# Filling TensorE's waits around normalizations and attention openings with products of resident constants

## The reference

```python
x = L0(x, ctx, ctx, mask)   # 16 heads of 64: softmax(q k^T / 8) v, out projection, + x
x = L1(x, ctx)              # gated fusion with the pooled ctx, then a layer normalization
x = L2(x, ctx, ctx)         # 16 heads of 16, relu projections, causal mask; normalization
x = L3(x, ctx)              # banded self-attention (window 64, per-head slopes) + norm,
                            # full cross-attention with ctx + norm, gelu feed-forward + norm
```

## Time and profile before

| | us |
|---|---|
| median of 3 runs | 1954.51 |
| lowest and highest | 1943.39, 1956.11 |
| the profiled execution | 1960.79 |
| its span (first to last instruction) | 1958.8 |
| TensorE matmuls busy | 1569.5 (80%) |
| TensorE weight loads busy | 829.0 (42%) |
| DVE busy | 939.8 (48%) |
| ACT busy | 736.4 (38%) |
| POOL busy | 253.6 (13%) |
| mean granted TensorE clock | 0.848 of full |

### The profile page before, as it was taken

One profiled execution on the slowest core, in us unless ns is written; L12 is line 12 of the kernel. 1 busy time (PEld: TensorE's weight loads), 2 busy tenths in 40 slices (PEclk: granted clock), 3 DMA queues, 4 the chain that ended last, 5 costly groups with the idle time before them and its releaser, 6 DMA issues.

```text
span 1958.8 us, 25869 instructions
## 1 busy us (share of the span) xinstructions
PE 1569.5 (80%) x8920; PEld 829.0 (42%) x8920; DVE 939.8 (48%) x2240; ACT 736.4 (38%) x1281; POOL 253.6 (13%) x116
## 2 busy tenths in 40 slices
PE   5998876688998887668899878676889987848686
PEld 2235544334424544533532554452353255536234
DVE  2654554461465464456155355445516626535551
ACT  1642333263263242427246215143524621514352
POOL 1012110200101211110010311120010031112001
PEclk9998787778999878867999877785899997879688
DMA  8001103402100211240210030223111012031200
GB/s 303 1 6 33 33 11 56 97 1 102 45 1 6 44 22 28 40 96 1 102 45 1 6 59 7 45 54 65 64 50 34 1 22 49 1 61 42 50 22 11
DMA packets 44860, 84.04 MB, mean 43 GB/s; under 512 B 10416, under 2 KB 28592, under 8 KB 44464
## 3 DMA queue, kind: packets, MB, share of 16 engines
q1 hardware_dynamic: 44288, 78.42, 17.0%
q10 hardware_dynamic: 432, 3.83, 0.5%
HBM read 42.37 MB, written 2.10 MB: 23 GB/s over the span
## 4 chain that ended last, share of the span: by engine, by line
PE 40%; issue 27%; DVE 18%; ACT 7%; SPq 4%; POOL 1%; DMA 1%; DVEq 0%; ACTq 0%; POOLq 0%
PE ring L1008 8%; DVE nmax L894 7%; PE ring L1029 5%; PE obank L1237 5%; PE ring L1218 4%; PE ring L1272 3%; DVE region_d L778 3%; ACT region_e L595 2%; SPq L377 2%; PE ring L1020 2%; ACT region_e L671 2%; SPq L370 2%; PE ring L1187 2%; PE ring L1039 2%; PE ring L1109 2%
## 5 line engine op out<-in xcount | busy, mean ns | idle before, releaser
L894 DVE TENSOR_REDUCE nmax<-ring 128x2 f32<-128x1024 f32 (+4 forms) x384 | 308.5, 852 | 253.3 <-PE ring L1187 179.5
L671 ACT ACTIVATE region_e<-ring 128x1024 f32<-128x1024 f32 (+4 forms) x384 | 267.4, 734 | 231.7 <-PE ring L1187 110.3
L778 DVE CUSTOM_DVE_ANT_0 region_d<-ring,maskb 128x512 f32<-128x512 f32 x256 | 165.7, 686 | 118.1 <-issue 117.8
L595 ACT ACTIVATE region_e<-region_d,nmin 128x512 f32<-128x512 f32 x256 | 182.6, 714 | 92.1 <-DVE nmin L778 86.1
L1187 PE MATMUL ring<-cbf 64*128 64x128 bf16 (+1 forms) x2048 | 177.4, 260 | 0.0
L663 ACT ACTIVATE q_all<-ring 2x1024 fp32r<-2x1024 bf16 x96 | 97.5, 1016 | 197.7 <-PE ring L1248 196.7
L1201 PE MATMUL ring<-k_tiles_a,q_all 64*128 64x512 f32 (+4 forms) x384 | 108.1, 578 | 65.6 <-DMA q_all<-q_parts 47.0
L1218 PE MATMUL ring<-q_all,k_tiles_a 64*128 64x512 f32 (+4 forms) x384 | 101.5, 531 | 72.6 <-ACT region_e L671 50.9
L1067 PE MATMUL obank<-region_e,vs 128*64 128x512 f32 x512 | 139.9, 630 | 15.1 <-DVE vs L764 15.1
L1057 PE MATMUL ring<-region_q 64*128 64x512 f32 x512 | 141.3, 636 | 5.4 <-ACT region_q L584 5.4
L529 POOL TENSOR_TENSOR nat_x<-nat_n,rows 128x1024 f32<-128x1024 f32 x16 | 39.0, 2439 | 641.6 <-DVE nat_n L859 641.6
(11 more groups left out here) (167 smaller groups left out, 2282.0 us busy)
## 6 DMA issues: line engine op xcount, KB each, us to landing
q_all<-q_parts SPq DMA_DIRECT2D x288, 64.0 KB, 2.3
k_tiles_a<-k_parts SPq DMA_DIRECT2D x144, 64.0 KB, 2.3
k_tiles_b<-k_parts SPq DMA_DIRECT2D x144, 64.0 KB, 2.3
region_b<-in_w_f SPq DMA_DIRECT2D x8, 1024.0 KB, 5.2
wvo<-in_wv SPq DMA_DIRECT2D x4, 1024.0 KB, 8.1
wqk<-in_wq SPq DMA_DIRECT2D x4, 1024.0 KB, 10.0
wqk<-in_wk SPq DMA_DIRECT2D x4, 1024.0 KB, 12.0
wvo<-in_wo SPq DMA_DIRECT2D x4, 1024.0 KB, 5.5
```

Source lines behind the costliest of these rows:

```text
L595: ins = act.activation(e0[:, n % E0, h, :], sm0[:, n % 2, h, :], ACT.Exp, bias=nmin0[:, n, h:h + 1], scale=-1.0, accum_out=sum0[:, n, h:h ...
L671: act.activation(e16[:, n % 4, 2 * u:2 * u + 2, 0:nq], slot((a, "B", g, kt, u))[:, :, 0:nq], ACT.Exp)\
L778: ins = dve.tensor_tensor_reduce(out=sm0[:, n % 2, h, :], in0=slot(("S0", p, kt))[:, h, :], in1=maskb[:, :], scale=-1.0, scalar=3.0e38, op ...
L894: dve.tensor_reduce(nmax[:, qt, 2 * u:2 * u + 2], slot(name)[:, :, 0:nk], AX.X, ALU.max, negate=True)\
```

## The change

A helper `keep_warm(n)` is added to TensorE's program. It issues n products of the constant `ident` (128x128, bf16) with the constant `keyrows` (128x512, bf16) into bank 0 of `obank`, with no wait and no semaphore. Nobody reads these results; the next group of heads that uses the bank begins with start=True. It is called with 18 products after the slot of a turn is free and before its transposes, with 5 after the transposes, and in `attention` with 6 at the opening, 2 after each first `pass_a` of `FULL`, 8 after those passes, and 6 before the first `pass_b`. This is 168 products per batch item: 92 around the four turns, 60 in the three attentions and 16 more in `FULL`. All 672 run on TensorE; the programs of DVE, ACT and SP are as before.

```diff
+                def keep_warm(n):
+
+                    for _ in range(n):
+                        pe.matmul(obank[:, 0, :], cb("ident", P), cb("keyrows", S), start=True, stop=True)
...
                 def turn(n, src):
 
                     dst = start(("X", n))
+                    if n:
+                        keep_warm(18)
                     for m in range(NT):
...
                 turn(1, nat_n)
+                keep_warm(5)
                 pe.wait_ge(*drained_by(("X", 1), b))
...
                 def attention(a):
+                    keep_warm(6)
                     for qt in range(NT):
                         for u in range(2):
                             pass_a(a, 0, qt, u)
+                            if a == FULL:
+                                keep_warm(2)
+                    keep_warm(8)
                     if a == BANDED:
                         pe.wait_ge(*drained_by(("VS", 1), b))
                         pe.wait_ge(ones_ready, b * 2 + 2)
                     for g in range(GROUPS):
                         for kind, *which in group_steps(g):
+                            if g == 0 and kind == "B" and which == [0, 0, 0]:
+                                keep_warm(6)
...
                 turn(2, nat_n)
+                keep_warm(5)
                 pe.wait_ge(*drained_by(("X", 2), b))
...
                 turn(3, nat_n)
+                keep_warm(5)
                 pe.wait_ge(*drained_by(("X", 3), b))
...
                 turn(4, nat_n)
+                keep_warm(5)
                 pe.wait_ge(*drained_by(("X", 4), b))
```

## The result

| | before | after |
|---|---|---|
| median of 4 runs each, us | 1955.31 (1943.39 to 1958.72) | 1925.01 (1919.54 to 1930.14) |
| ratio after / before | | 0.9847, 95% interval 0.981 to 0.9884 |
| profiled execution; its span, us | 1960.8; 1958.8 | 1930.1; 1928.2 |
| mean granted TensorE clock | 0.848 | 0.913 |

Predicted were 1924 us and a ratio of 0.984. The span is 30.6 us shorter. The two profiled executions both lie above the median of their kernel, by 5.5 and 5.1 us.

A forecast was written before the change was run, and what follows sets the result against it. TensorE's slow products at the low clock after waits were taken to be on the path behind each normalization. Terms 2.8 + 1.8 + 1.2 - 0.3 + 2.2 = 7.7 us per item, times 4 = 31 us, gave 1924 us, range 1904 to 1951.

The forecast's parts named there:

- turn(4): Before F1: transposes 0.4 us shorter, F1 at the high clock 13.9 us for 16.31; gain 2.8 us per item.
- turn(2): Before KS: 2.3 us if the clock holds over the unfilled rest, perhaps half if it falls; taken as 1.8 per item.
- turn(3) and FULL's opening: Before QC and in FULL: 1.7 through SP's queue, 1.4 lost in A passes, 0.5 and 0.4 gained; 1.2 us per item.
- the step that stops at group 0: In FULL: 0.4 us taken for group 0; no gain counted in the later groups, since nothing is added there.
- turn(1) and CAUSAL's opening: Around Q2: 1.0 us gained, as DVE waited only 1.02; 6 products at the opening delay all by 1.3; net -0.3.
- CAUSAL: Group 0 of CAUSAL: 3.4 us if the clock holds through 15 us of interleaved work, weighed with 0.65; 2.2 per item.
- transposes don't count as work: Rival at the turns: clock falls between the 18 products and the projection, turns win nothing, groups win; 1950 us, chance 0.08.
- The openings give back what they can win: Rival in the attentions: clock holds behind the turns, but the attentions fall back; 3.2 us per item, 1942 us, chance 0.27.
- The clock then holds much longer: Rival in FULL: later groups, partly at 0.5, hold the clock too; 12 us per item, 1906 us, chance 0.13.
- Slower: Rival at the turns and openings: constant products don't hold the clock and overrun the waits; 2020 us, chance 0.07.

The follow-up runs named there:

- e1: The changed kernel with all 672 added products kept, each with one moving column in place of 512; 1953.22 us, ratio 1.0004.
- e3: The changed kernel with added products only in the attentions, none at the turns; 1954.5 us, ratio 1.0007.
- e8: The changed kernel with only the 18 products at the four turns, without the 5 behind the transposes and none in the attentions; 1931.6 us, ratio 0.9889.
- e2: The changed kernel with only the 18 and 5 products at the four turns, none in the attentions; 1926.37 us, ratio 0.9862.
- e7: The changed kernel with 10 products for 18 at turn(1), and in the attentions only CAUSAL's 8 and 6 ahead of its first B pass; 1918.8 us, ratio 0.982.
- e9: e7 plus one product ahead of every B pass but the first of each group of FULL; 1915.07 us, ratio 0.9822.
- e12: e9 without the product in group 0, so only in groups 1 to 3 of FULL; 1907.41 us, ratio 0.9778.
- e11: e7 plus 28 products in BANDED's wait for the stacking DMAs, between the first and second B pass; 1920.16 us, ratio 0.9837.
- e5: The changed kernel without the 2 products behind each first A pass of FULL; 1920.57 us, ratio 0.9837.
- e4: The changed kernel without any added product inside FULL; 1921.27 us, ratio 0.9837.

## Why the prediction was right

The time, 1924 us forecast against 1925.01 measured, was right, and so was the mechanism: with their columns the products gain 1.5%, without them nothing (e1). Two of the five terms were near their size. The other three were wrong in both directions, and that they cancelled was luck.

- **turn(4), 2.8 per item forecast, 2.5 measured,** in every run with the 18 and none without (e3's column has +0.1). F1 took 14.00 us; 13.9 was forecast.
- **turn(2), 1.8 forecast, 2.4 measured.** The clock held over the rest of the wait, 1.98 us, so the full 2.3 came and not the half that I had weighed in. By e8 the five products behind the transposes are what holds it.
- **turn(3) and FULL's opening, 1.2 gained forecast, 1.1 lost measured.** The limits up to group 0 were right: SP's queue holds the first A pass, and the query DMAs close up to the key DMAs; but 0.7 came through on average and not 1.7, since a block of key DMAs took longer (1.4 to 1.5 came through in e2, e7, e9 and e12). The pairs cost 1.3 where 1.4 was forecast, and group 0 became 0.9 shorter, as forecast (0.5 + 0.4). What failed is the step that stops at group 0: I had carried groups 1 to 3 as unchanged. Group 1 took 18.2 or 18.3 us in three of the four items of after, where the kernel before has 15.7 in three and 18.7 in one, and in the other item groups 1 and 2 lost 2.7 together, because values ran at the low clock. This can happen without the products in FULL (e11), but with them it happened in every item.
- **turn(1) and CAUSAL's opening, 0.3 lost forecast, 1.1 lost measured (+1.5 and -0.4).** The mis-sized term is the 18 products at 4.0 us. Ahead of them stand one-column products, the clock is at 0.68 over the stretch, and the 17 that are recorded took 5.52. Since three of four items of e2, e5 and e8 show no loss with the same 18, its size is uncertain.
- **CAUSAL, 2.2 gained forecast, 5.0 measured.** 3.4 weighed with 0.65 was too careful. The clock held, and first B to first B fell to 10.5 us; 12 was forecast. The added products there also raised the clock in the seven passes ahead of group 0 and in the groups behind it, which no term had.

Thus the last two misses give 2.0 us per item more than forecast, turn(2) and turn(4) together 0.3 more, and turn(3) with FULL 2.3 less: the total came out right with errors of more than 2 us per item in its parts.

Of the rivals, "transposes don't count as work" falls with its time of 1950 and its step that the turns win nothing: they win nearly all. The page "TensorE: Matmul & The Clock Gate" of the Trainium skill says in Part 4 that transpose mode "doesn't count as PE-busy the same way"; whether that holds here stays open. In e8 the clock lasted through eight transposes and a wait of 1.54 us, and F1 began at the high level; at turn(2), with 4.5 us of waits and transposes between full products, it fell as KS began, in three of four items. That transposes don't hold the clock would fit both. "The openings give back what they can win" was half right: e2 and after can't be told apart in time, so the products in the attentions together are worth nothing that can be measured. It was given 0.27, and its time of 1942 was wrong because it put the losses of the openings against no gain: CAUSAL wins 4.5 us per item more in after than in e2, CAUSAL's opening and FULL lose 1.2 and 2.9. "The clock then holds much longer" didn't happen in after. e9 and e12 show that where it is made to happen, only the last group gains by it. "Slower" falls: at turn(4) the transposes start with the end of the 18 as forecast, and only turn(1) overran by more.

Open stays where exactly the clock's changes fall in an execution. With it stay open the loss at turn(1) and the 2.5 to 3 us in FULL's group 1, which come and go between items and runs with the same instructions at that place, and why the opening's products bring the second every time. Comparisons of e4 to e7 with after are within their intervals.

## What to carry to other kernels

Fill a known wait of TensorE with products that need nothing and stream full columns, where a projection on the path follows it, sized (here 0.22 us each at the high clock) to end about with the wait, and with a few more behind the transposes where a wait remains. In stages where TensorE waits for DVE and ACT between its passes, as in FULL's middle groups, a higher clock brought nothing, and products between passes were pure cost at the low clock: leave them out, except where TensorE is busy almost throughout, as in the last group. Judge by the stages' ends and the time, not by the mean clock, which rose from 0.848 to 0.891 in e3 with no gain at all. And compare a stage item by item before a mean over items is believed.

## What the runs showed of the hardware that I had not expected

- In e1, 18 products of one column took 0.59 us together and did not hold the clock: the wait behind them stood at 0.55.
- In e9, TensorE was busy for 11.76 of 13.5 us in FULL's group 0 and stayed at 0.50. Most of that was passes of 64 rows with short waits between them. In after's opening, where pairs of full products stand between such passes, it came to 1.00. The fewest products that do this were not looked for.
- A stretch with the same instructions (FULL's group 1, e11 against e7) took 3.0 us more, from transposed maxima to transposed maxima 18.7 us (871.30 to 889.97) in place of 15.7 (867.18 to 882.86), more than a turn gains. The 28 products ahead of it aren't needed for that, since e7's fourth item has 18.6 without them; whether they helped, one profile of each can't say.
- A product of 512 bf16 columns took 0.22 us at the high clock with f32 work around it, 3.83 us for 17. At the low clock two took 1.04 us (849.06 in after's timeline) and a single one in e9 0.6, so 0.43 from start to start, near the 0.44 taken from the masks' products; what a single one costs beyond that is small but stands in full on the path.
